# A transformer layer with a routed feed-forward, on one core: the five hand-written orders are laid anew among neighbours

## The chip, the core and the metric

The program runs on one core of a Trainium2 chip. The core has five engines that run their own instruction streams in order: TensorE (PE, matrix products; its weight loads are listed apart as PEld), VectorE (DVE), ScalarE (ACT), GpSimd (POOL) and SyncE (SP), which issues DMAs. They wait for one another through semaphores only. The metric is device time in microseconds. Three runs of the kernel before gave 949.52, 950.03 and 952.06; their median is 950.03 us.

## The reference

Eight images of 1024 tokens with 29 features go through one layer, all in float32:

```python
h = x.reshape(8, 1024, 29) @ W + pe                       # tokens, width 128
z = layernorm(h)
Q, K, V = z @ Wq + bq, z @ Wk + bk, z @ Wv + bv           # 8 heads of 16
attn = softmax((Q @ K.T + causal_mask) / 4)               # causal, 1024 x 1024 per head
h = h + (attn @ V) @ Wo + bo
f = layernorm(layernorm(h)) * ln_scale + ln_bias
shared = swiglu(f @ shared_in.T) @ shared_out.T + b       # hidden width 256
g = argmax(f @ group_gate.T + ...)                        # 2 groups of 4 experts
top-2 of softmax(expert logits of group g), renormalised
he = swiglu(f @ expert_in.T)                              # one hidden layer for all experts
h = h + shared + sum_e weight_e * (he @ expert_out[e].T) + expert biases
```

## The kernel before

**Tiling.** Images are numbered i = 0 to 7. An image has two halves of 512 tokens, and a half has four tiles of 128. Attention of an image is cut into four units (UNITS, four heads times one half of the queries each).

**Steps.** All work is a list of small steps. Each has a letter, which names its stream:

- s, `score` (L546): one 128-query tile of one head against up to 512 keys, 96 steps an image. DVE takes the row maximum from the bank: with the causal mask on the diagonal (L784), without it elsewhere (L780). Two banks, so PE may be two scores ahead of DVE.
- t, `turn` (L559): the maxima of a unit are transposed, split on DVE (L798 to L804) and put into q_stack by SP (L449).
- p, `prob` (L576): keys against queries again, now transposed and with the maximum subtracted, 96 steps an image. ACT takes the exponential into one of four slots `pt` (L1051). Two banks again. On the diagonal POOL zeroes the masked part (`prob` on POOL, L1213), once for each group of four.
- w, `weigh` (L594): four heads' probabilities times values; `take` on ACT (L1042) empties the bank after a unit.
- e, `emb` and a, `stat1`, `turn1`, `ztl`, `q`, `k`, `rest_of`, `v`: embedding and what comes ahead of attention (L508, L516, L480 to L482, L529 on PE; L720 to L770 on DVE; L1023 to L1032 on ACT; L1186 to L1207 on POOL). POOL's `v` (L1194) adds the output bias to h.
- b: behind attention: `to` (L612; L816 and L818 on DVE), `ant` (L616; L1061 on ACT), `oproj` (L622; L825 on DVE), `stat2`, `z2t` (L628; L843, L1067, L1069, L1229), `gates` (L632), `route` parts 0 to 4 on DVE (L872 to L923), `counts` (L638).
- f: `in` (L480 to L482 into bank_f; tanh on ACT L1089, then L936 or L945 on DVE), `hid` (L1097 and L1234), `expert` (L682 to L684; ACT L1107, DVE L955). h: `shared` (L645, L648; DVE L961). c: `combine` (four L1113 on ACT, then L1243, L1247, L1249 on POOL). d, i: transfers of queries and keys, first loads and weights.

**The order.** `streams(i)` gives for every letter the steps of image i in a fixed order, `works` says which engine has a part in a step, and the table `ORDER` holds one string of letters per engine. `woven` takes, letter by letter, the next step of that stream. So a step never passes another of its own letter, but it may stand anywhere among the others, and on each engine at a place of its own. Attention of image i+1 is interleaved with the feed-forward of image i.

**Waits.** Each step waits for the semaphores that it needs. Steps of many kinds on PE write the one bank bank_m; whichever is next waits until the one ahead was taken (`m_free`, counters `m_ready` and `m_taken`). `fill` puts products into the PE stream that nothing reads: ahead of the first steps, one ahead of each of the first scores, and ahead of the last half's `oproj` (5), `z2t` (14) and `gates` (6). A fp32 product is two rows of the trace.

Of the kernel before, what the change touches and what calls it, by code (L numbers as in the profile page):

```python
# [118 lines left out]
def works(engine, i, st):  # L119
# [15 lines left out]
    if engine == "pool":  # L135
# [8 lines left out]
        "eeaaaaessessssassssassssssesssstssasssasssssssssspsspptpssspspppswspasppsspwspsasssppwppssaspspwsspappss"  # L144
        "spspspwppspspspspwptswwassssssspspbpssppbwpspsbsppsapspswssppsspssppswsppsbppspssppappspwwpsstspspwsspas"
        "psbpsswpspspsppspfpswpspfspsafpspfsptspwwwpspsfssppfspspwpspsbppsfspfsppwwpspsfppsbfpspsfspfspsfssppfsps"
        "hssppwwsppsapspsssfssfspswstpswspsasspsswsppsesppspstspsspwpsbpssspsppsspsppspbspspswwwssbwspsbppsspapps"
        "wwpsbsspspbspfpfptsspfpwpwppssfsasfspfpsfspfspsfssfssbwsbspfbssppfsspbspfssbsppsfpspptwwsphpwspbspwpsbpp"
        "sappfppfppfbwwpefpspfsppfssppwppwppsfpspspfpsappsfppsfspafspshsspfspptfswwwpsspfbpsspfbsfbsppsfssbppsfsp"
        "spawsppwspwwpspasppswpsptpssppeppswwppsbspswspsaspsffspbpfsappffpsswspfspfpfbwssppfpspbfbpsspfbfsspbpspf"  # L150
        "sshppssfppbswwswsspptfsppsffppssbspspfsppsfspfsappswwspwspfspspftwspswppsffpsspapspsfpspsasfpssapsfpssbf"
        "spshsftspspfssfpssesfspwwwwsppapspspwspsppassppsswsppsspspswpspwsppsbsppspwpspspbpwpspsptspwpspbpspswsbp"
        "pspspeppspwpspasppwpsspwbspwsspbpspfspfpspffapswwsbfpbfpspbsfpsfbppsfbspspfpsphssppfbfssftspsfssbsppsfsa"
        "sfsppfspasswwwwsppfsppfsstppfpsapsspfsfppssasppsfpssfpspswwwwssppfspspbfpspsfspshpsspwpssfsppsfpspstffsp"
        "sfsspesswwwppssbsppspspbpsspwsppwpspbpsspbpwspwpeppssppaspwpsppspwspptwsppsbswssassfspfafsspfppsbpfspafs"
# [1197 lines left out]
```

## Time and profile before

| | before |
|---|---|
| median of 3 runs | 950.03 us |
| profiled execution | 951.46 us |
| its span | 949.7 us |
| mean granted TensorE clock | 0.984 |
| PE, DVE, ACT, POOL busy | 96%, 83%, 63%, 39% |

The profiled execution took 951.46 us, of which its span (first to last instruction) is 949.7 us and 1.8 us lie around it. PE is busy nearly throughout, so the windows by stage and the waits say more than the shares; they stand in the section of rows.

### The profile page before, as it was taken

Reading aid. Unit: us, or ns where it says so; the run is one execution under the profiler, and the core shown is the slowest. Engines: PE = TensorE matmul, PEld = TensorE weight load, DVE = VectorE, ACT = ScalarE, POOL = GpSimd, SP = SyncE. Lnnn points to the kernel's source line nnn. Section 1 sums busy time; section 2 is a strip of 40 time slices with the busy share of each in tenths; the row PEclk is TensorE's granted clock in tenths of the full one; section 3 lists DMA queues with packets and bytes.
Section 4 is the critical chain, followed back from the end, with each engine's and each line's share of the span. In section 5 each row is a group of like instructions: output and inputs, shape, how many; then the busy total and the mean of one; then the engine's idle time right before and its main releaser. Section 6 shows DMA issues by size and latency. Waiting matters only on the chain. (4 is left out here: it accounts for less than half of the span.)

```text
span 949.7 us, 17664 instructions
## 1 busy us (share of the span) xinstructions
PE 907.3 (96%) x5646; PEld 540.7 (57%) x5646; DVE 786.0 (83%) x2529; ACT 596.3 (63%) x1365; POOL 374.8 (39%) x526
## 2 busy tenths in 40 slices
PE   7788999899999999999999999999999999999996
PEld 7633356356575656457555756466564765555575
DVE  5799988798789888889889889898889998894543
ACT  1335675475857675775766675675767576776644
POOL 3713323323445335343354325344444234332424
PEclk9799999899999999999999999999999999999999
DMA  5231011200111001110102001110110101000000
GB/s 178 59 54 50 20 35 34 65 16 4 34 46 57 10 18 49 38 65 18 35 15 72 26 24 40 45 47 30 38 46 17 47 26 46 26 13 2 12 1 23
DMA packets 45980, 35.19 MB, mean 37 GB/s; under 512 B 10816, under 2 KB 44608, under 8 KB 45760
## 3 DMA queue, kind: packets, MB, share of 16 engines
q1 hardware_dynamic: 43680, 31.97, 10.5%
q10 hardware_dynamic: 2208, 2.10, 1.0%
q8 instruction: 45, 0.74, 0.4%
q14 instruction: 47, 0.39, 0.1%
HBM read 4.28 MB, written 4.19 MB: 9 GB/s over the span
## 5 line engine op out<-in xcount | busy, mean ns | idle before, releaser
L1051 ACT ACTIVATE pt<-bank_p 128x512 f32<-128x512 f32 (+3 forms) x768 | 349.9, 492 | 200.6 <-PE bank_p L576 178.5
L784 DVE CUSTOM_DVE_ANT_0 bank_s<-bank_s,causal 128x384 f32<-128x384 f32 (+3 forms) x512 | 244.3, 505 | 40.0 <-PE bank_s L546 37.2
L546 PE MATMUL bank_s<-k_stack,q_stack 96*128 96x512 bf16 (+3 forms) x768 | 236.0, 333 | 17.4 <-DVE mx L784 8.9
L576 PE MATMUL bank_p<-q_stack,k_stack 99*128 99x512 bf16 (+3 forms) x768 | 229.0, 332 | 6.9 <-ACT pt L1051 5.1
L780 DVE TENSOR_REDUCE mx_far<-bank_s 128x1 f32<-128x512 f32 x256 | 166.0, 682 | 20.6 <-PE bank_s L546 19.2
L1213 POOL TENSOR_SCALAR_AFFINE_SELECT pt<-pt 128x512 f32<-128x512 f32 x128 | 81.1, 636 | 206.7 <-ACT pt L1051 206.5
L594 PE MATMUL bank_w<-pt,v 128*32 128x512 f32 (+3 forms) x1536 | 155.2, 502 | 0.2 <-POOL pt L1213 0.2
L546 PEld LDWEIGHTS bank_s<-k_stack,q_stack 96*128 96x128 bf16 x768 | 72.1, 99 | 131.9 <-DVE mx L784 55.6
L576 PEld LDWEIGHTS bank_p<-q_stack,k_stack 99*128 99x128 bf16 x768 | 72.7, 99 | 117.6 <-ACT pt L1051 69.8
L682 PE MATMUL bank_f<-wex_h,hid_h 128*128 128x512 f32 x256 | 116.4, 455 | 0.8 <-DVE gate L936 0.7
L684 PE MATMUL bank_f<-wex_h,hid_l 128*128 128x512 f32 x256 | 101.4, 396 | 0.0
L683 PE MATMUL bank_f<-wex_l,hid_h 128*128 128x512 f32 x256 | 101.2, 395 | 0.0
L1113 ACT ACTIVATE sel<-sel,wsel 128x128 f32<-128x128 f32 x256 | 81.5, 399 | 15.5 <-DVE sel L955 15.5
L784 DVE DVE_READ_ACCUMULATOR2_ANT mx<- 128x1 f32 x512 | 72.0, 141 | 0.0
L594 PEld LDWEIGHTS bank_w<-pt,v 128*32 128x32 f32 x1536 | 36.4, 109 | 62.5 <-issue 47.4
L1243 POOL TENSOR_TENSOR sel<-sel 128x256 f32<-128x256 f32 x64 | 46.8, 731 | 59.4 <-ACT sel L1113 59.4
L1107 ACT ACTIVATE sel<-bank_f,gm 128x512 f32<-128x512 f32 x64 | 44.0, 687 | 41.5 <-PE bank_f L684 21.8
L480 PE MATMUL bank_f<-z2t_h,win_h 128*128 128x512 f32 x128 | 66.6, 520 | 3.3 <-DVE gate L936 2.0
L1234 POOL TENSOR_TENSOR hid_l<-hid,hid_h 128x512 fp32r<-128x512 f32 x32 | 41.0, 1284 | 71.9 <-ACT hid_h L1097 71.9
L955 DVE SCALAR_TENSOR_TENSOR sel<-bank_f,gm,sel 128x512 f32<-128x512 f32 x64 | 47.7, 746 | 26.1 <-PE bank_f L684 16.5
L682 PEld LDWEIGHTS bank_f<-wex_h,hid_h 128*128 128x128 f32 x256 | 48.4, 189 | 13.2 <-issue 1.4
L684 PEld LDWEIGHTS bank_f<-wex_h,hid_l 128*128 128x128 f32 x256 | 48.1, 188 | 11.2
(139 smaller groups left out, 1428.9 us busy)
## 6 DMA issues: line engine op xcount, KB each, us to landing
q_stack<-qk_h SPq DMA_DIRECT2D x96, 64.0 KB, 2.6
k_stack<-qk_h SPq DMA_DIRECT2D x84, 64.0 KB, 2.6
q_stack<-qk_m SPq DMA_DIRECT2D x64, 64.0 KB, 2.6
out<-h SPq DMA_DIRECT2D x16, 256.0 KB, 2.4
k_stack<-qk_m SPq DMA_DIRECT2D x56, 64.0 KB, 2.6
q_stack<-qk_l SPq DMA_DIRECT2D x32, 64.0 KB, 2.6
k_stack<-qk_l SPq DMA_DIRECT2D x28, 64.0 KB, 2.4
x_sb<-x_t SPq DMA_DIRECT2D x16, 64.0 KB, 2.4
```

The source lines that it names most:

```text
L480: nc.tensor.matmul(dst, wh, xh, start=True, stop=False)
L546: nc.tensor.matmul(s_bank[s % 2][:, 0:cols], q_stack[0:STACK, half, hd, t % HT * P:(t % HT + 1) * P], k_stack[0:STACK, hd, key_place(i, ha ...
L576: nc.tensor.matmul(p_bank[p % 2][:, q0:HALF], k_stack[:, hd, key_place(i, kt // HT), kt % HT * P:(kt % HT + 1) * P], q_stack[:, half, hd, ...
L594: mm = nc.tensor.matmul(w_bank[VW * j:VW * (j + 1), q0:HALF], v[:, i % 2, kt, first:first + VW], pt[:, k % PT_SLOTS, j, q0:HALF], start=(k ...
L682: nc.tensor.matmul(f_bank[g][:], hid_h[:, c, tok], wex_h[:, c, w], start=(c == 0), stop=False)
L683: nc.tensor.matmul(f_bank[g][:], hid_h[:, c, tok], wex_l[:, c, w], start=False, stop=False)
L684: mm = nc.tensor.matmul(f_bank[g][:], hid_l[:, c, tok], wex_h[:, c, w], start=False, stop=(c == HID // P - 1))
L780: nc.vector.tensor_reduce(mx_far[:, u, col:col + 1], s_bank[s % 2][:], AX.X, ALU.max).then_inc(s_taken, 1)
L784: nc.vector.tensor_tensor_reduce(src, src, causal[:, HALF - cols:HALF], 1.0, -3.0e38, ALU.add, ALU.max, mx[:, u, col:col + 1]).then_inc(s_ ...
L1051: nc.scalar.activation(pt[:, k % PT_SLOTS, j, q0:HALF], p_bank[p % 2][:, q0:HALF], ACT.Exp, scale=0.25).then_inc(exp_done, 1)
L1113: nc.scalar.mul(sel[:, t % 2, part], sel[:, t % 2, part], wsel[:, t, e:e + 1]).then_inc(weighted, 1)
L1213: nc.gpsimd.affine_select(out=d, in_=d, compare_op=ALU.is_ge, fill=0.0, base=0, pattern=[[0, G4], [1, P]], channel_multiplier=-1).then_inc ...
```

## The change

Only the table `ORDER` differs. Each of its strings holds the same letters as before, so every product, wait, buffer and transfer is there as before. Counting the steps whose place in their engine's list differs, and the mean distance over all steps of the engine: PE 1123 of 2224 (0.82 places), DVE 426 of 1301 (0.47), ACT 429 of 1142 (0.56), POOL 158 of 318 (0.87), SP 80 of 123 (1.4). Runs of one letter change little: on PE a run of two p's stands 160 times before and 176 times now.

```diff
     "pe": (
-        "eeaaaaessessssassssassssssesssstssasssasssssssssspsspptpssspspppswspasppsspwspsasssppwppssaspspwsspappss"
...
+        "eeaaaaesesssssassssasssssssessstssssassssssssssptspppsspspsspsssppwpppasswpspsaspssppsspasswpsspaspsps"
...
     "sp": (
-        "ieedededtdetdtdddttddddtcddtdetddctddtdctdddetddtcdtedctdddeedtddtdctecddtdddtdtddctdddtedcddteteddcddtt"
...
+        "eiededdtdtddtddtddtddetcteddeddtdctddtdctdddtedddtectdedcdtdeddtddcdttddecteddddtdcdttdddtdcddttddectddet"
...
```

At the start of DVE's stream, the split of the query and key weights (L967, L970) and the first steps of image 0; z is the normalised half. Before:

```order
L967 CAST wqk_h<-z 128x128 x2
L970 TENSOR_TENSOR wqk_l<-z,wqk_h 128x128 x2
L720 TENSOR_TENSOR h<-bank_m,pos_sb 128x512
L726 BN_STATS stats<-h 128x6 x4
L732 BN_AGGR mv<-stats 128x2 x4
L738 TENSOR_SCALAR z<-h,mv,rs 128x128 x4
L720 TENSOR_TENSOR h<-bank_m,pos_sb 128x512
```

Now:

```order
L720 TENSOR_TENSOR h<-bank_m,pos_sb 128x512
L726 BN_STATS stats<-h 128x6 x4
L732 BN_AGGR mv<-stats 128x2 x4
L720 TENSOR_TENSOR h<-bank_m,pos_sb 128x512
L967 CAST wqk_h<-z 128x128 x2
L970 TENSOR_TENSOR wqk_l<-z,wqk_h 128x128 x2
L738 TENSOR_SCALAR z<-h,mv,rs 128x128 x4
```

The weight split moved from ahead of the first embedding to behind the second, and the second embedding moved ahead of the normalisation L738, which it followed. On SP the load of image 1's first half now stands ahead of the ten loads of the remaining weights, and on ACT the fill of three key rows (L1138) stands first instead of between `q` and `k` of the second half.

Near the end of PE's stream, in image 7: two `in` steps, the last two `weigh` steps (L594) and the first `expert` step. Before:

```order
L480 MATMUL bank_f<-z2t_h,win_h 128x512
L481 MATMUL bank_f<-z2t_h,win_l 128x512
L482 MATMUL bank_f<-z2t_l,win_h 128x512
L594 MATMUL bank_w<-pt,v 32x256 x4
L594 MATMUL bank_w<-pt,v 32x128 x4
L480 MATMUL bank_f<-z2t_h,win_h 128x512
L481 MATMUL bank_f<-z2t_h,win_l 128x512
L482 MATMUL bank_f<-z2t_l,win_h 128x512
L682 MATMUL bank_f<-wex_h,hid_h 128x512
```

Now:

```order
L480 MATMUL bank_f<-z2t_h,win_h 128x512
L481 MATMUL bank_f<-z2t_h,win_l 128x512
L482 MATMUL bank_f<-z2t_l,win_h 128x512
L480 MATMUL bank_f<-z2t_h,win_h 128x512
L481 MATMUL bank_f<-z2t_h,win_l 128x512
L482 MATMUL bank_f<-z2t_l,win_h 128x512
L594 MATMUL bank_w<-pt,v 32x256 x4
L594 MATMUL bank_w<-pt,v 32x128 x4
L682 MATMUL bank_f<-wex_h,hid_h 128x512
```

`in` step (3,1) moved ahead of the two `weigh` steps. At the same place of DVE's stream, the gate products L936 and L945 of the `in` steps, `route` part 4 (L914 to L923) and the first `to` (L816, L818). Before:

```order
L936 SCALAR_TENSOR_TENSOR gate<-gate,bank_f 128x512
L914 TENSOR_TENSOR topp<-eprob,top 128x16
L915 TENSOR_REDUCE esum<-eprob 128x4
L917 TENSOR_REDUCE tsum<-topp 128x4
L919 SCALAR_TENSOR_TENSOR tden<-esum,tsum 128x4
L921 RECIPROCAL trec<-tden 128x4
L923 TENSOR_TENSOR wsel<-topp,trec 128x16
L945 SCALAR_TENSOR_TENSOR hid<-gate,bank_f 128x512
L936 SCALAR_TENSOR_TENSOR gate<-gate,bank_f 128x512
L945 SCALAR_TENSOR_TENSOR hid<-gate,bank_f 128x512
L816 RECIPROCAL rec<-bank_m 128x16
```

Now:

```order
L945 SCALAR_TENSOR_TENSOR hid<-gate,bank_f 128x512
L936 SCALAR_TENSOR_TENSOR gate<-gate,bank_f 128x512
L945 SCALAR_TENSOR_TENSOR hid<-gate,bank_f 128x512
L914 TENSOR_TENSOR topp<-eprob,top 128x16
L915 TENSOR_REDUCE esum<-eprob 128x4
L917 TENSOR_REDUCE tsum<-topp 128x4
L919 SCALAR_TENSOR_TENSOR tden<-esum,tsum 128x4
L921 RECIPROCAL trec<-tden 128x4
L923 TENSOR_TENSOR wsel<-topp,trec 128x16
L816 RECIPROCAL rec<-bank_m 128x16
```

The six routing instructions moved behind both L945. POOL's `v` of the last half (L1194) moved 35 places back, behind the last `combine` of image 6.

In the middle of POOL's stream, where image 5's first masks (L1213) begin: a `combine` (L1243 to L1249) and a `rest_of` (L1205, L1207). Before:

```order
L1213 AFFINE_SELECT pt<-pt 128x4x128 x2
L1243 TENSOR_TENSOR sel<-sel 128x256
L1247 TENSOR_TENSOR h<-h,sel 128x128
L1249 TENSOR_TENSOR h<-h,sel 128x128
L1213 AFFINE_SELECT pt<-pt 128x4x128 x4
L1205 CAST qk_m<-qk_r 128x512
L1207 TENSOR_TENSOR qk_l<-qk_r,qk_m 128x512
```

Now:

```order
L1243 TENSOR_TENSOR sel<-sel 128x256
L1247 TENSOR_TENSOR h<-h,sel 128x128
L1249 TENSOR_TENSOR h<-h,sel 128x128
L1213 AFFINE_SELECT pt<-pt 128x4x128 x2
L1205 CAST qk_m<-qk_r 128x512
L1207 TENSOR_TENSOR qk_l<-qk_r,qk_m 128x512
L1213 AFFINE_SELECT pt<-pt 128x4x128 x3
```

The combine stands ahead of image 5's first mask, and the rest_of ahead of its third mask instead of behind the fifth.

## Rows read from the trace of the kernel before

**Rows 1.** Windows: stretch, length, then busy us (instructions) of PE, PEld, DVE, ACT, POOL; clock, DMA share, GB/s.

```profile
0.00:200.00 200.00, 177.26 (x1028) 97.96 (x1028) 165.41 (x527) 98.51 (x204) 73.04 (x94) 0.93 0.21 59
200.00:880.00 680.00, 671.00 (x4289) 399.58 (x4289) 588.93 (x1916) 462.75 (x1074) 273.58 (x389) 1.00 0.10 33
...
897.00:919.00 22.00, 22.00 (x146) 19.64 (x144) 9.03 (x23) 7.14 (x16) 7.44 (x12) 1.00 0.04 14
```

**Rows 2.** Groups by form: busy us, mean ns of one, idle before.

```profile
L1051 ACT ACTIVATE pt<-bank_p 128x512 f32<-128x512 f32 x384 | 216.7, 601 | 91.6 <-PE bank_p L576 84.8 <-PE bank_w L594 5.5
L780 DVE TENSOR_REDUCE mx_far<-bank_s 128x1 f32<-128x512 f32 x256 | 166.0, 682 | 20.6 <-PE bank_s L546 19.2
```

**Rows 3.** Timeline of the start: start us, length, engine, instruction, idle before.

```profile
5.67 0.36 DVE L967 CAST wqk_h<-z 128x128 fp32r<-128x128 f32 x2 [1.64 <-DMA bk_sb<-bk]
...
6.07 0.49 DVE L970 TENSOR_TENSOR wqk_l<-z,wqk_h 128x128 fp32r<-128x128 f32 x2
...
7.65 2.05 PE L508 MATMUL bank_m<-tokw_sb,x_sb 128*128 128x128 f32 x8 [0.95 <-DVE h L720]
...
10.40 1.12 DVE L738 TENSOR_SCALAR z<-h,mv,rs 128x128 f32<-128x128 f32 x4 [1.58 <-POOL rs L1190]
...
12.27 0.63 PE L516 MATMUL bank_m<-ident,z 128*128 128x128 f32 x4
```

**Rows 4.** Timeline, the first two scores and the embedding behind them.

```profile
25.46 0.27 PE L546 MATMUL bank_s<-k_stack,q_stack 96*128 96x128 bf16 x1 [0.83 <-DMA k_stack<-qk_l]
...
26.06 0.31 PE L546 MATMUL bank_s<-k_stack,q_stack 96*128 96x128 bf16 x1
...
28.22 0.69 DVE L720 TENSOR_TENSOR h<-bank_m,pos_sb 128x512 f32<-128x512 f32 x1 [1.99 <-PE bank_m L508]
```

**Rows 5.** Windows of two stretches in image 1's scores.

```profile
181.70:188.50 6.80, 6.60 (x36) 2.56 (x36) 2.59 (x12) 1.55 (x4) 0.63 (x1) 0.50 0.22 70
165.00:180.00 15.00, 12.63 (x70) 4.85 (x66) 14.71 (x38) 7.60 (x19) 8.38 (x12) 1.00 0.22 73
```

**Rows 6.** Timeline of image 5's second and third mask, the third's use, a rest_of.

```profile
607.97 0.64 POOL L1213 TENSOR_SCALAR_AFFINE_SELECT pt<-pt 128x512 f32<-128x512 f32 x1 [1.26 <-ACT pt L1051]
...
610.84 0.64 POOL L1213 TENSOR_SCALAR_AFFINE_SELECT pt<-pt 128x512 f32<-128x512 f32 x1 [2.24 <-ACT pt L1051]
...
612.35 0.64 PE L594 MATMUL bank_w<-pt,v 128*32 128x256 f32 x8
...
615.25 0.61 POOL L1205 CAST qk_m<-qk_r 128x512 bf16<-128x512 f32 x1
615.95 1.16 POOL L1207 TENSOR_TENSOR qk_l<-qk_r,qk_m 128x512 bf16<-128x512 f32 x1
```

**Rows 7.** Timeline around the last two weigh steps.

```profile
894.41 1.27 POOL L1234 TENSOR_TENSOR hid_l<-hid,hid_h 128x512 fp32r<-128x512 f32 x1
894.45 0.86 PE L594 MATMUL bank_w<-pt,v 128*32 128x256 f32 x16
894.62 0.60 ACT L1089 ACTIVATE gate<-bank_f 128x512 f32<-128x512 f32 x1 [0.38 <-PE bank_f L482]
894.70 1.01 DVE L923 TENSOR_TENSOR wsel<-topp,trec 128x16 f32<-128x16 f32 x1
...
895.63 0.68 DVE L945 SCALAR_TENSOR_TENSOR hid<-gate,bank_f 128x512 f32<-128x512 f32 x1
...
896.36 0.50 PE L480 MATMUL bank_f<-z2t_h,win_h 128*128 128x512 f32 x1 [1.05 <-DVE hid L945]
...
897.16 0.39 PE L682 MATMUL bank_f<-wex_h,hid_h 128*128 128x512 f32 x1
```

**Rows 8.** L923 in all: ns min, median, max; first and last start.

```profile
L923 DVE TENSOR_TENSOR wsel<-topp,trec x16: 174/175/1019, 143.6 to 930.8; 128x16 f32<-128x16 f32 x16
```

**Rows 9.** POOL's `v` in all, and DVE's use of the last product of attention.

```profile
L1194 POOL TENSOR_TENSOR h<-h,bo_sb x16: 1263/1288/1327, 15.5 to 796.7; 128x512 f32<-128x512 f32 x16
...
904.94 0.69 DVE L825 TENSOR_TENSOR h<-bank_m,h 128x512 f32<-128x512 f32 x1 [2.54 <-PE bank_m L622]
```

More of the change, by code:

```diff
@@ new lines @@
+        "hspspwwsppsaspsspsfssfsswstswppspsapsssswspspesswppspstsspspppsppssbsppssppppspsbssswwssbwssbspwpspappsp"
+        "wsppbswssbpsfpsspfpftpwpfpspswpsfssapsfpfspsfpsfssfssbwsbspfbpsspfspspbsfpssbspfppsstwpspwphpwpsbswpsbpp"
+        "sappfppfppfbwwpsfpepfpspsfpspwppwppsfpspsfpspasppfppfspsapsfphssfpspstfswwwspspfbsspfpsbfpspsbfspsbsppsf"
+        "psawpwssppwwppsaspspwpspstpsppeppswwppsbspswspsaspsffbspfpsafspfsppwpfsspfpfwspspbfsbpspfbssppfbfpssbspf"
+        "psphwsspfbpsspwwsppstfspsfpfppssbppssfpsspfpsfspapswwspspfswsppftspwpspwpsfasspfpspsfpsapssfspsapssfbpsp"
@@ new lines @@
+        "fsshspsfstfssfppsespfswwwwsppsapssppwpspspassppsswspspssppswssppwpspbspsppwppsspbpwpspstppswpspbsppswsbp"
+        "pspspepspspwppaspspwsppwbpswsspbppfspsfssppfapwwpbfsfbpfssbpfppsfbspfbpspfsppshspfpsbfssftssfpssbsppsfsp"
+        "sapsffpssaswwwwspspfppfssptpfsspasppfsfpspsaspsfpspsfspspwwwwsppsfsbppsfpsspfspsphpsspwssfsppstfpssffpss"
+        "fssppesswwwpspsbspspsppbspspwppbpspwspsbpspspwwpeppssppasppwspsppwsptspwpspbswssassffspapfpsfsbpspffassp"
+        "pfspswpspfwpssbfsbfbspspfbspfbpspsfpphspspfbpswwpssptwspsfspbspspfppsapspfpspswpspswwsppfpfssppftssppfsp"
@@ new lines @@
+        "sappsswwwsppsfsppsfspspfpspaspsfsspfsppsassppfbfsshsspfstfspsfssefspswwppswwspsaspsspswspspasppswpspbpps"
+        "swsppbppspsptpwspspbwpspsbpssppasppwsppwppsasppwpbsppswssbspsfppswpfbspfbspfppbfppsfbsfpsfpsbfppsshpspfb"
+        "ssfssbfpsptfesswwppsswwspsfbppssfppsfasppsffpssppapspsfspwwwssptfsppawspspfspsfpsspapspsfppswwspsfwspspf"
+        "tppsfspsfpspshppssfsppsfppssfssfpspsfspesswwwwssppspssppsbppwpspbpwsppsapswspsppbswsbppssppstppwppsapwpp"
+        "spsppwpspbspswpssaspsfsfppsbspffsspefspspfassppfwwwssppbffspsbfbpspsfbpssfsspphspfsspptfpssbpsspffsapsww"
@@ new lines @@
+        "fssssbsbsstbshsssbbfabsbfffsbssfsfessfssfsafssfasashsssfstssafbsssbssfssbsbfssabssssssastssesssssssasffb"
+        "sbfssffbsfsabfsfbssabssfsbssbsbssfbhsssfsssstassfssfssfssbssfsfssbassbstfsfbsbfssasfssssassasfssssfshsst"
+        "ssfseafssassssassssssssssssassssbsssbsstsssssbssbesssbasssssbbssfsbfbsbafafsbfsfbsfssafbsbfssbhssssfssst"
+        "ssfssbsbsbsabsbfssasfsfsstsfsfsasfssfsssssasfssfsssssfssshssssftssfssssfessasssbssbssasssbbssesssbsassst"
+        "ssssssasfsfasffssbfssasfbsbbsffsbsbsfbsassfbbssbhssasssstfsssssbbssbssfssfasfssfsstssfsfbsabssssfssfsssf"
@@ new lines @@
+        "sasssfasssfshssstssfsseafssasssssssasssassbsssbssstssssbsbsassbassssssbsbbsbfsfbbffsbsfsfssffsbbssbhsfss"
+        "sssbstfbssebabssssbfssasfssassfsfsasfstssfssassfsfssssssafsfstssfssshssfssssfsssssfesassssssabssbsssasss"
+        "ssbssbtssbsasssssssasfsfssbfssfebssfbsfsbfabsfsssbabfssssafssshssstssbfsbssfbasssssssassftfssbssbssbbsba"
+        "ssfsfsfssfssssssfsassfsfsssssfstsshsssssfssssfssbssbsssssbbstsssssbssssssbssbfsbfbfbfssfssfssfssfsssfsss"
+        "fsstbbbbbhfbfbbbffffffffbbfbbbhbfffbfbfbffffbffbffhff"
@@ L199 @@
+        "cfapacccpaacppcpppppppapbabfafappbcbpcpfafpcacpccppcaapppcpbppppbaaffabapcbpcppfcafcpapacpcapcppapppcpbp"
+        "pbffabpabcapcppfafcpcpaccpcapappppppbppcbaaffaaccppbpbpfapcfpapcppccppppcpbppcbffppppbcbcpppfpfccabccbff"
         "cccccc"
```

73 lines of the change are left out of this document (24 added, 49 removed).

## Prediction

> **What bounds the kernel now.** I read three views in this order: the windows by stage, the timelines of the places whose order changes, and the groups by form. The windows show that from 200 to 880 us PE is busy 671.0 of 680 us, so 9.0 us are idle there, and that it is busy all of 897 to 919 [rows 1]. In the first 200 us it is busy 177.26, so 22.7 us are idle, with DVE busy 165.41. So three quarters of the program is bound by PE's own work, which the change leaves as it is (the same products, in another order). What an order can win lies in the idle 22.7 us of the first 200, the 9.0 us of the middle, and a few us at the end. One more loss is no idle time: from 181.7 to 188.5 us the granted clock is 0.50, PE's lower level of 1.2 GHz, and PE is busy 6.60 us with what 3.3 us would do at the full 2.4 GHz [rows 5]. Ahead of it, from 165 to 180, PE was busy only 12.63 of 15 us while DVE was busy 14.71: a stretch in which DVE is the bound.
>
> **Scale.** The profiled execution took 951.46 us (span 949.7 and 1.8 around it), 1.43 above the median 950.03 of the runs. The sum is made on 951.46, and 1.43 is taken off at the end. What the measurement of this kernel can tell from no change is about 0.3%, 2.85 us.
>
> **The change, part by part.**
>
> *Start.* (a) The split of the weights, L967 and L970, runs from 5.67 to 6.56, 0.89 us, ahead of everything else on DVE [rows 3]. It now stands between the second L720 and L738. The first L720 gains nothing by this, since it waits for PE's first product; so the split loses a place where it stood beside that product. PE's second product ends at 9.70 (7.65 + 2.05), and DVE can take its L720 (0.69 us, as at 28.22, [rows 4]) from about 9.8, ending near 10.45, when the factors that L738 waited for until 10.40 are there too. The split then ends at 11.35, and L738 (1.12) at 12.5, against 11.52 before (10.40 + 1.12). PE's L516 stood at 12.27 behind fill products, so it moves to about 12.65: +0.37 us. (b) Before, the second embedding of image 1 began on PE 0.10 us behind the second score of 26.06. Now it stands behind the first, of 25.46: 0.60 us sooner, and DVE had been idle 1.99 us for it until 28.22 [rows 4]. The score moved back costs PE the same where it now stands, so this gains 0.60 only while DVE is what is late, which it is there: -0.6. (c) On SP, the load of image 1 goes ahead of ten loads of weights, which are used twenty us later; on ACT, the fill L1138 goes to an idle start. I count both as 0. Together the start gives -0.2 us; the bounds are +0.4 (only a) and -0.6 (only b).
>
> *The first 200 us otherwise.* Steps there move by about one place on all engines. The far row maximum L780 takes DVE 682 ns and a score needs less on PE; the exponential L1051 takes ACT 601 ns [rows 2]. Where more than two scores stand together on PE, each further one costs up to 0.68 us of waiting for DVE, and each further p up to 0.60 for ACT. I counted runs in both tables: scores beyond the second in a run fall from 29 to 26 in the whole program, -2.0 us at most; p's beyond the second rise from 4 to 7, +1.8 us at most. The two bounds nearly cancel, and other steps stand beside each of these runs in either order: I take 0. DVE's own order is the same in the stretch from 165 to 180, apart from PE's, so I expect its 2.37 us of idle PE (15 - 12.63), and the half clock behind it, to come again [rows 5]. Term 0. The ends: if both go, -2.37 - 3.3 = -5.7 us; if a second such stretch comes, +3.3 with about 2 us of idle time ahead, +5.3.
>
> *The middle.* 9.0 us idle in 680 leave little to win; half of it would be -4.5, and I see no part of the change that collects it. Of what could be lost, the nearest is on POOL, which now has `combine` and `rest_of` ahead of masks that they followed. In image 5, `rest_of` (0.61 + 1.16, from 615.25 to 617.11, 1.86 us) stands ahead of the third mask. That mask began at 610.84 and the one before ended at 608.61 (607.97 + 0.64), so 2.23 us lie open, the 1.86 fit with 0.37 to spare, and the products that use the mask began at 612.35, 0.87 us after it ended at 611.48 [rows 6]. By DVE's order its input is made ahead of the second mask, so it can start at once. So it costs 0; the other end is its whole 1.86. I read the similar places (`combine` ahead of the first mask of image 5, and in image 6) the same way. SP's transfers move by 1.4 places on average; PE's idle 9.0 us leave little room for any wait on them now, and I take 0, with the 1.86 as the nearest size of a loss.
>
> *The end.* Before, DVE did the six instructions of `route` part 4 between L936 and L945 of one `in` step. The last of them, L923, took 1.01 us beside POOL's L1234 (894.41 to 895.68), while its median is 0.175 us [rows 7, 8]. L945 so came at 895.63, and PE's next `in` product, which writes the bank that L945 empties, waited 1.05 us, until 896.36; the last `weigh` had ended at 895.31 (894.45 + 0.86), and the first `expert` product came at 897.16. Now six routing instructions stand behind both L945, and `in` (3,1) ahead of the two `weigh` steps. L945 of (2,1) can come right behind its L936, near 893.5, its L945 be done by 894.2, and the product of (3,1) follow (3,0) without a gap, near 894.5 to 895.3. The `weigh` products (0.86 for the last of them) then end near 896.1. The bank that `expert` writes is emptied behind the gate of (3,0): L1089 until 895.22 (894.62 + 0.60), then L936, as long as L945's 0.68, near 896.0. So `expert` can start at 896.1 instead of 897.16: -1.06 us. From 897 to 919 PE has no idle time [rows 1], so the gain is carried on.
>
> What was moved back has a price too. `route` part 4 is done near 897.8 instead of 895.71 (894.70 + 1.01), and `combine` on ACT and POOL waits for its weights. POOL's `v` of the last half, 1.29 us, stands behind the last `combine` of image 6 now, and is needed by DVE's last L825, at 904.94 [rows 9]. ACT is busy 7.14 and POOL 7.44 of the 22 us from 897 on [rows 1], so both have room: by my count `v` is done near 903, a good 0.8 us before L825 now wants it (904.94 - 1.06 = 903.9), and I take 0. If it is late, it costs up to its own 1.29, which would turn the end into +0.2. So the end lies between -1.06 and +0.2; I take -1.06, as each time of it stands in a row.
>
> A rule of the Trainium skill bears on L923. The row: 1.01 us beside a POOL operation that reads two tiles, 0.175 us at the median of 16 [rows 7, 8]. By "SBUF — State Buffer" (Who interferes with whom) a DVE instruction with two inputs in SBUF and a GpSimd instruction that reads SBUF exclude each other for the whole instruction, and issue order decides who waits. The trace agrees with that here. By the rule, routing moved behind both L945 may meet the next POOL operation in turn, and lose the same 0.84 again; that would be -0.9 for the end instead of -1.1, since only 0.2 of it is on PE's path. The sum below doesn't use it.
>
> **The sum.** Start -0.2, first 200 us otherwise 0, middle 0, end -1.1: -1.3. On the profiled execution 951.46 - 1.3 = 950.2; on the median's scale 950.03 - 1.3 = 948.7 us.
>
> **The rivals.**
>
> *A, the forecast: 948.7, its own range 946.5 to 951.0.* The two placed terms come as worked out and the rest nets out to within 2 us.
>
> *B, faster: the DVE-bound stretch dissolves.* Where PE's order around 165 us puts other work between scores, PE gets back the idle 2.37 and the half clock, 3.3 us, doesn't recur: 948.7 - 5.7 = 943.0. For it: PE's order changes in half of its steps, and 22.7 us of idle time in the first 200 are a large store. Against it: DVE is busy 14.71 of 15 us there and its order is the same, so PE can't get its scores taken sooner. A part of it (the half clock alone) gives 945.4.
>
> *C, slower: a mask comes late.* The place is image 5's third mask behind `rest_of`. If that pair starts later than 609.85 (the mask must start by 612.35 - 0.64 = 611.71, less 1.86), the `weigh` products wait. At worst 1.86 us, and if a half-clock stretch like that of 181.7 follows the gap, 3.3 more: 948.7 + 1.86 + 3.3 = 953.9. For it: 0.37 us to spare is less than what steps move. Against it: the products have 0.87 us more, and a short gap in the middle left the clock at 1.00 before.
>
> *D, the gain isn't there: 950.0.* The 1.06 us at the end is taken back by `v` or `combine` behind it, and the start nets to 0. Then the change does nothing that can be measured.
>
> **Chances.** A 0.42, B 0.25, C 0.22, D 0.11. The bounds of 0.3% lie at 947.2 and 952.9. A falls below 947.2 with 0.11 and is the same with 0.31; B is faster with 0.25; C is slower with 0.20 and the same with 0.02; D is the same with 0.08, slower with 0.03. So faster 0.36, same 0.41, slower 0.23. The range reaches from B's full size to C's: 943.0 to 954.5, with about 0.1 left out at either side.
>
> **What would show it.** Start: L516 of the first half near 12.65, and DVE's wait for the second embedding of image 1 down from 1.99 by 0.6. First 200 us: granted clock 0.50 again for some 6 us behind a stretch from 165 on with DVE at 14.7 of 15. Middle: PE busy near 671 of 680 and no new wait of L594 for POOL's L1213 beyond 0.2 us. End: no idle time of PE between `in` (2,1) and `expert`, which start about 1.1 us sooner relative to 880. The forecast is wrong if the idle time of PE in the first 200 us moves by over 2 us from 22.7, or if a half-clock stretch comes or goes.

## The result and the profile after

Over 20 runs of each, the changed kernel takes 944.43 us in the median (941.3 to 950.8) and the kernel before 950.75 (948.5 to 953.0). The ratio is 0.9944, with a 95% interval of 0.9932 to 0.9956: 5.3 us less (4.2 to 6.5). The forecast was 948.7, within its range of 943.0 to 954.5. The sign and the range held, and the size did not: I had -1.3 us.

The profiled execution took 945.19 us, its span 943.4 us, at a mean granted clock of 0.983 (before 0.984). In the mean of the 20 runs it is 0.983 too, and 0.983 in 86 runs of the kernel before, so the clock isn't what made it faster. Windows of the changed kernel, columns as in [rows 1]; 200 to 880 answers to the row of before there, and 891 to 913 to that of 897 to 919:

```profile
0.00:200.00 200.00, 177.99 (x1034) 97.63 (x1035) 166.79 (x534) 99.04 (x206) 74.53 (x95) 0.93 0.23 61
200.00:880.00 680.00, 673.89 (x4307) 400.71 (x4305) 589.98 (x1919) 467.84 (x1084) 273.89 (x389) 1.00 0.10 33
...
891.00:913.00 22.00, 22.00 (x146) 19.58 (x145) 9.89 (x29) 8.78 (x20) 9.76 (x16) 1.00 0.04 14
```

PE's idle time from 200 to 880 us fell from 9.0 to 6.1 us, in a stretch where I had written 0. To see where time went I set each PE step of one trace against the same step of the other, and took the median difference of the steps in each stretch. A positive number means later than in before:

| steps near (us of before) | changed kernel |
|---|---|
| 25 to 50 | 0.0 (from -0.3 to +0.8) |
| 65 to 77 | +2.5 |
| 100 to 180 | +1.0 to +0.6 |
| 200 | -1.5 |
| 255 | -1.9 |
| 260 | -2.7 |
| 565 | -3.7 |
| 570 | -4.9 |
| 605 | -5.5 |
| 640 to 890 | -5.7 to -5.3 |
| 895 to the end | -6.3 |

The curve falls in steps, with long flat parts between them. The steps at 260, 570, 605 and 895 each stand at one gap of PE in the trace of before. Between 260 and 565 it falls by another 1.0 us, in small pieces at no large gap. The first three of these gaps, with the ACT instruction ahead of two of them (timeline of before, columns as in [rows 3]):

```profile
258.00 0.69 ACT L1032 ACTIVATE qk_h<-bank_m,bk_sb 128x512 bf16<-128x512 f32 x1
...
258.58 0.44 ACT L1051 ACTIVATE pt<-bank_p 128x128 f32<-128x128 f32 x2
...
259.00 0.38 PE L576 MATMUL bank_p<-q_stack,k_stack 99*128 99x512 bf16 x1 [0.68 <-ACT pt L1051]
...
569.57 1.17 POOL L1207 TENSOR_TENSOR qk_l<-qk_r,qk_m 128x512 bf16<-128x512 f32 x1
569.75 1.02 DVE L923 TENSOR_TENSOR wsel<-topp,trec 128x16 f32<-128x16 f32 x1
...
571.82 0.34 PE L546 MATMUL bank_s<-k_stack,q_stack 96*128 96x384 bf16 x1 [0.99 <-DVE mx L784]
...
605.91 0.69 ACT L1032 ACTIVATE qk_h<-bank_m,bq_sb 128x512 bf16<-128x512 f32 x1 [1.30 <-DMA q_stack<-qk_l]
...
607.03 0.34 PE L576 MATMUL bank_p<-q_stack,k_stack 99*128 99x384 bf16 x1 [0.92 <-ACT pt L1051]
```

At 258 us ACT evacuates k, 0.69 us, ahead of an exponential that PE waits for, and PE stands 0.68 us. At 570 the last instruction of `route` part 4 takes 1.02 us beside POOL's L1207, as it did near 895 beside L1234 [rows 7, 8]. At 606 ACT waits 1.30 us for a transfer with exponentials queued behind it. A fourth gap of the same size stands at 297, where PE waits 0.74 us for the transfer `q_stack<-mrow_l`. The changed kernel has it too (0.70), so it is in neither's favour. The same places in the changed kernel:

```profile
566.08 0.17 DVE L923 TENSOR_TENSOR wsel<-topp,trec 128x16 f32<-128x16 f32 x1
566.17 0.42 DVE L784 CUSTOM_DVE_ANT_0 bank_s<-bank_s,causal 128x256 f32<-128x256 f32 x1
566.33 0.74 POOL L1243 TENSOR_TENSOR sel<-sel 128x256 f32<-128x256 f32 x1 [2.44 <-ACT sel L1113]
...
566.93 0.34 PE L546 MATMUL bank_s<-k_stack,q_stack 96*128 96x384 bf16 x1
...
600.37 0.69 ACT L1032 ACTIVATE qk_h<-bank_m,bq_sb 128x512 bf16<-128x512 f32 x1 [0.67 <-DMA q_stack<-qk_l]
...
601.49 0.34 PE L576 MATMUL bank_p<-q_stack,k_stack 99*128 99x384 bf16 x1 [0.36 <-ACT pt L1051]
```

L923 is back at 0.17, with no POOL instruction beside it, and the score behind it has no idle time. The gap at 606 is down to 0.36. The end of attention, which answers to [rows 7]:

```profile
889.33 0.60 ACT L1089 ACTIVATE gate<-bank_f 128x512 f32<-128x512 f32 x1 [0.23 <-PE bank_f L482]
889.56 0.40 PE L482 MATMUL bank_f<-z2t_l,win_h 128*128 128x512 f32 x1
889.88 0.86 PE L594 MATMUL bank_w<-pt,v 128*32 128x256 f32 x16
889.96 0.69 DVE L936 SCALAR_TENSOR_TENSOR gate<-gate,bank_f 128x512 f32<-128x512 f32 x1 [1.03 <-ACT gate L1089]
...
890.79 0.47 PE L682 MATMUL bank_f<-wex_h,hid_h 128*128 128x512 f32 x1
```

`in` (3,1), the weigh products and `expert` follow without idle time. `expert` starts at 890.79, against 897.16 before. All of 6.37 us less the 5.3 that steps at 880 had is 1.07: the term of the end as forecast, 1.06.

### The profile page after: what moved, and what is told of

Its sections match the earlier page's. It is cut to its first block, busy times and chain, and to the rows that moved or that the text cites. A ratio compares the mean times of both kernels' runs of the same rounds, so it can differ in the third digit from the quotient of the medians.

```text
span 943.4 us, 17664 instructions
## 1 busy us (share of the span) xinstructions
PE 905.6 (96%) x5646; PEld 539.0 (57%) x5646; DVE 785.6 (83%) x2529; ACT 597.1 (63%) x1365; POOL 376.1 (40%) x526
## 4 chain that ended last, share of the span: by engine, by line
PE 85%; DVE 9%; ACT 2%; issue 1%; DMA 1%; SPq 0%; ACTq 0%; POOL 0%; POOLq 0%; DVEq 0%
PE bank_w L594 13%; PE bank_p L576 13%; PE bank_s L546 13%; PE bank_f L682 6%; PE bank_f L683 6%; PE bank_f L684 6%; PE bank_f L480 3%; PE bank_f L482 3%; PE bank_f L481 3%; PE bank_m L648 3%; DVE bank_s L784 3%; DVE mx_far L780 3%; PE bank_m L508 2%; PE bank_m L622 2%; PE bank_m L612 1%; PE bank_m L632 1%
## 5 line engine op out<-in xcount | busy, mean ns | idle before, releaser
L546 PE MATMUL bank_s<-k_stack,q_stack 96*128 96x512 bf16 (+3 forms) x768 | 238.8, 336 | 15.6 <-DVE mx L784 7.5
L1213 POOL TENSOR_SCALAR_AFFINE_SELECT pt<-pt 128x512 f32<-128x512 f32 x128 | 82.1, 642 | 217.5 <-ACT pt L1051 217.4
L594 PE MATMUL bank_w<-pt,v 128*32 128x512 f32 (+3 forms) x1536 | 154.7, 497 | 0.3 <-ACT ot L1042 0.2
L684 PE MATMUL bank_f<-wex_h,hid_l 128*128 128x512 f32 x256 | 101.3, 396 | 0.0
L1234 POOL TENSOR_TENSOR hid_l<-hid,hid_h 128x512 fp32r<-128x512 f32 x32 | 41.1, 1285 | 108.4 <-ACT hid_h L1097 108.4
L1243 POOL TENSOR_TENSOR sel<-sel 128x256 f32<-128x256 f32 x64 | 46.9, 733 | 59.4 <-ACT sel L1113 59.4
L594 PEld LDWEIGHTS bank_w<-pt,v 128*32 128x32 f32 x1536 | 35.4, 108 | 59.2 <-issue 45.7
L684 PEld LDWEIGHTS bank_f<-wex_h,hid_l 128*128 128x128 f32 x256 | 48.1, 188 | 11.2
```

The lines of the kernel that those rows point to most:

```text
L546: nc.tensor.matmul(s_bank[s % 2][:, 0:cols], q_stack[0:STACK, half, hd, t % HT * P:(t % HT + 1) * P], k_stack[0:STACK, hd, key_place(i, ha ...
L594: mm = nc.tensor.matmul(w_bank[VW * j:VW * (j + 1), q0:HALF], v[:, i % 2, kt, first:first + VW], pt[:, k % PT_SLOTS, j, q0:HALF], start=(k ...
L684: mm = nc.tensor.matmul(f_bank[g][:], hid_l[:, c, tok], wex_h[:, c, w], start=False, stop=(c == HID // P - 1))
L1213: nc.gpsimd.affine_select(out=d, in_=d, compare_op=ALU.is_ge, fill=0.0, base=0, pattern=[[0, G4], [1, P]], channel_multiplier=-1).then_inc ...
```

## The experiments

The difference that moves the time is small, so two measures stand side by side: the ratio of many runs, and the curve of steps of one trace. Where two programs have the same order the curve mostly stays level within 0.1 us over hundreds of us. It isn't always so: waits for a transfer come and go between traces of the same order. The one at 297 stands in the trace of before and not in e3's. One of 0.97 us at 506 stands in e1's trace and one of 0.79 in e7's, and in neither before nor e3. A step of one trace at such a place is not an effect of the order.

The ratio is an estimate of its own over the runs, and not the quotient of the two means (for e1 that quotient is 0.9985, for e9 0.9983). e3, e5 and e6 ran once each, for the trace, so of them only steps are read. The others (mean and standard deviation of the times, ratio to before with its interval, number of runs):

| kernel | mean us | sd | ratio | runs |
|---|---|---|---|---|
| before | 950.7 | 1.1 | | over 80 |
| changed | 945.3 | 2.6 | 0.9944 (0.9932 to 0.9956) | 20 |
| e1, new up to 200 us | 949.3 | 2.3 | 0.9979 (0.9964 to 0.9994) | 12 |
| e7, new up to 57 us | 949.7 | 1.7 | 0.9992 (0.9979 to 1.0005) | 12 |
| e8, new from 57 to 200 | 950.7 | 2.9 | 0.9999 (0.9979 to 1.0019) | 12 |
| e2, new from 200 to 880 | 948.5 | 1.3 | 0.9979 (0.9968 to 0.9990) | 12 |
| e12, four single moves | 947.7 | 0.8 | 0.9967 (0.9956 to 0.9978) | 12 |
| e9, changed without these | 948.9 | 2.8 | 0.9976 (0.9962 to 0.9990) | 12 |
| e10, changed, 57 to 200 old | 947.0 | 0.9 | 0.9962 (0.9950 to 0.9974) | 5 |
| e4, changed with fills | 945.5 | 1.7 | 0.9944 (0.9927 to 0.9960) | 6 |
| e11, changed with 4 swaps | 946.5 | 3.0 | 0.9958 (0.9939 to 0.9977) | 12 |

Within a kernel the time follows the clock of the run: over the 20 runs of the changed kernel the fastest took 941.3 us at a clock of 0.989 and the slowest 950.8 at 0.973. One line through all runs, with a level for each kernel, gives 0.47 us for each 0.001 of clock (0.3 to 0.7 in one kernel alone, and no slope in e12's runs). Where "at equal clock" stands below, the level of this line at 0.984 is meant, with two standard errors.

**By stretches.** e1, e2 and e3 take the new orders in one stretch each. In each string of `ORDER` a piece is taken from the new table only where it holds the same letters as the old one, so all else stays. e1:

```diff
     "pe": (   # all pieces up to 200 us, on all five engines
-        "eeaaaaessessssassssass...
+        "eeaaaaesesssssassssass...
```

> The kernel before with the new orders of all engines only up to 200 us (the places are taken by the times of its trace), the old ones behind. Theory G (gaps: the change wins by gaps of PE that vanish at single places, most of them behind 200 us): this kernel stands within 2 us of before, with steps at 200 us from 0 to 1.6 us earlier and no difference that grows behind. Rival C (clock: the change wins by half-clock stretches of the first 200 us that shrink): the whole gain is here, 4 to 6 us.

Measured 0.9979, -2.0 us (-3.4 to -0.6), and -1.3 +- 0.6 at equal clock. That is within the 2 us of theory G and far from C's 4 to 6. C falls: the gain is not all in the first 200 us. G's second sign is not borne out: in e1's trace, which is of its slowest run, the steps at 200 us come 0.6 later than in before, and not 0 to 1.6 sooner.

e2 has the pieces from 200 to 880 us:

```diff
-  pieces of before, 200 to 880 us
+  pieces of the changed kernel, 200 to 880 us
   (but POOL: ..."apcpp", the piece that moves v(7,1), as before)
```

> The kernel before with the new orders only from 200 to 880 us, without the one long piece of POOL's order that moves the last v. Theory G: the PE gaps at 258.3 (0.68), 570.8 (0.99) and part of that at 606.1 (0.92 to 0.36) vanish, steps at 880 us come 3.0 to 3.8 us earlier than in before when the first 200 us are set equal; the time falls by about 3.5 us, 0.37%. Rival C: 0 to 1 us. My prediction on record had 0 for this stretch.

The steps at 880 us come 3.2 us sooner than in e3, whose orders there are the old ones, when both are set equal at 200 us. The gaps at 258 and 571 are gone, and that at 606 is 0.69. The time fell by 2.0 us (3.0 to 1.0), at equal clock 2.3 +- 0.6. So G holds in kind, with a size from 2.0 (times; 2.3 at equal clock) to 3.2 us (steps of one trace), at the lower end of its 3.0 to 3.8 or below it. My 0 for the middle is wrong by either.

e3 has the new orders from 880 us on (42 letters), without the move of v. The part at 895:

```diff
-  PE  ... w w in(3,1) expert        DVE ... route4 in(2,1) in(3,0) in(3,1)
+  PE  ... in(3,1) w w expert        DVE ... in(2,1) in(3,0) in(3,1) route4
```

> The kernel before with the new orders only from 880 us on. By the forecast's term of the end the first expert product behind the last weigh comes 1.06 us sooner relative to steps at 875 us, and stays so to the end; route part 4's L923 takes 0.175 us. If the place of POOL's v mattered (it is not moved here), the end would differ from the changed kernel's by more than 0.2.

The steps behind 895 us come 0.98 us sooner relative to those at 880. The end of the changed kernel has 1.0 too, so the place of v gives and costs nothing.

**Single moves.** e5 puts four single moves, each of one engine alone, into the kernel before; 12 letters differ:

```diff
 ACT, 258 us:   - k(2,1)  prob(23,2)
                + prob(23,2)  k(2,1)
 POOL, 569 us:  - rest_of(0,1) hid(0) hid(1) prob combine(6) rest_of(1,1) combine(7)
                + hid(0) combine(6) rest_of(0,1) hid(1) combine(7) prob rest_of(1,1)
 ACT, 603 us:   - take(3) prob(0,3) prob(1,0)
                + prob(0,3) prob(1,0) take(3)
 DVE, 894 us:   - route(0,4) in(2,1) in(3,0) in(3,1)
                + in(2,1) in(3,0) in(3,1) route(0,4)
```

> The kernel before with four single moves of the change, each on one engine alone, so that each place speaks for itself. (1) ACT near 258 us: the evacuation of k (L1032, 0.69) behind one exponential instead of ahead of it; theory: PE's gap of 0.68 is just this length and goes; rival: it needs the moves of PE too and stays. (2) POOL near 569 us: hid and combine ahead of rest_of; theory: L923 was slow (1.02) only because rest_of's L1207 ran beside it, so it takes 0.175 now and PE's gap of 0.99 shrinks by 0.85; rival: the gap is of DVE's order (route ahead of the gate product), and stays over 0.8. (3) ACT near 603 us: two exponentials ahead of take; theory: PE's gap of 0.92 at 606 falls by up to 0.56; rival: it hangs on the transfer of queries that L1032 waits for (1.30), and stays. (4) DVE near 895 us: route part 4 behind the gate products of in; theory: PE's gap of 1.05 goes with this alone, and expert comes 1.06 sooner.

Against e3 the curve falls by 0.62 at 258, 0.97 at 571 and 0.41 at 606, and against before by 1.00 at 895. Between these places it is level within 0.1 us (for instance -3.10 at 260 and -3.19 at 560). Timeline of e5 at 567 us and at 891 us:

```profile
566.60 0.18 DVE L921 RECIPROCAL trec<-tden 128x4 f32<-128x4 f32 x1
566.67 0.28 PE L546 MATMUL bank_s<-k_stack,q_stack 96*128 96x256 bf16 x1
566.81 0.17 DVE L923 TENSOR_TENSOR wsel<-topp,trec 128x16 f32<-128x16 f32 x1
566.90 0.68 DVE L936 SCALAR_TENSOR_TENSOR gate<-gate,bank_f 128x512 f32<-128x512 f32 x1
...
890.05 0.86 PE L594 MATMUL bank_w<-pt,v 128*32 128x256 f32 x16
890.84 0.50 PE L480 MATMUL bank_f<-z2t_h,win_h 128*128 128x512 f32 x1
...
891.68 0.47 PE L682 MATMUL bank_f<-wex_h,hid_h 128*128 128x512 f32 x1
```

DVE's order at 567 is that of before, only POOL's differs, and L923 takes 0.17 us instead of 1.02: the slow instruction was a matter of what POOL did beside it. The other traces say the same: with POOL's old order there it took 1.02 us in all seven, and with the new one under 0.19 in all seven. Near 891 PE's order is that of before (`weigh` ahead of `in`), only DVE's differs, and the gap of 1.05 us is gone all the same. The page "SBUF — State Buffer" of the Trainium skill (Who interferes with whom) has a DVE instruction with two SBUF inputs and a GpSimd instruction that reads SBUF shut each other out. The trace agrees: 1.02 and 1.01 us beside L1207 and L1234, 0.174 to 0.177 in all 16 executions of the changed kernel. The size of the step at 606 is less sure than the other three. The gap there is 0.55 to 0.97 us in the seven traces with ACT's old order, and 0.35 to 0.69 in six with the new one. The same kernel traced again (e12) has it at 0.60 and a step of 0.15, where e5 has 0.35 and 0.41.

e6 gives the other engines' parts of the same places to the kernel before:

```diff
 PE, DVE, ACT, 566 to 571 us: as changed; POOL as before
 SP: the piece of 15 transfers of images 5 and 6 as changed
 PE, 895 us:    - weigh(22) weigh(23) in(3,1)
                + in(3,1) weigh(22) weigh(23)
```

> The kernel before with the other engines' parts of the same places. (1) PE, DVE and ACT near 566 to 571 us as in the change, POOL as before: if the slow L923 beside POOL makes the gap, something of it stays (over 0.4, L923 or another instruction long); if DVE's order does, it goes. (2) SP's piece of 15 transfers of images 5 and 6 as in the change: by the rival of the transfer, ACT's wait of 1.30 for q_stack<-qk_l near 606 falls to 0.7 and PE's gap from 0.92 to near 0.4; by the theory of ACT's order nothing changes. (3) PE alone near 895 us, in (3,1) ahead of the two weigh: L945 still stands behind the slow route part, so PE waits for it ahead of in, and the weigh products come behind: expert 0.8 to 0.9 us later than in before.

(1) The gap at 571 stays, 0.98 us, and L923 takes 1.02: the rival of DVE's order falls. (2) The gap at 606 stays at 0.80 and ACT's wait for the transfer at 1.2, so it isn't SP's order of transfers. (3) The steps behind 895 come 2.5 us later than at 880, three times what I expected. Timeline and windows of e6 there:

```profile
894.78 1.00 DVE L923 TENSOR_TENSOR wsel<-topp,trec 128x16 f32<-128x16 f32 x1
...
896.44 0.50 PE L480 MATMUL bank_f<-z2t_h,win_h 128*128 128x512 f32 x1 [1.83 <-DVE hid L945]
...
897.34 0.95 PE L594 MATMUL bank_w<-pt,v 128*32 128x256 f32 x16
...
898.22 0.79 PE L682 MATMUL bank_f<-wex_h,hid_h 128*128 128x512 f32 x1
898.39 0.59 ACT L1042 COPY ot<-bank_w 128x512 f32<-128x512 f32 x1 [2.93 <-PE bank_w L594]
898.87 1.28 ACT L1113 ACTIVATE sel<-sel,wsel 128x128 f32<-128x128 f32 x4
899.24 0.63 PE L684 MATMUL bank_f<-wex_h,hid_l 128*128 128x512 f32 x1
```

```profile
894.60:897.30 2.70, 0.87 (x4) 0.49 (x3) 2.35 (x4) 0.75 (x2) 1.15 (x1) 1.00 0.00 0
897.30:901.00 3.70, 3.70 (x24) 2.52 (x24) 0.69 (x1) 1.77 (x5) 0.73 (x1) 0.59 0.02 4
```

Behind 1.83 us of idle PE the mean granted clock is 0.59 over 3.7 us. Within it the clock stands at 0.50, its lower level, for 3.41 us from 897.97 on, and L684 takes 0.63 us instead of 0.40. e9's trace has the same (1.88 us idle, then 3.41 us at 0.50). Behind the gap of 1.05 in before, the clock stayed at 1.00 [rows 1]. So of the 2.5 us that PE's move costs without DVE's, 0.8 is the longer gap (1.83 less 1.05), and 1.7 is the work that PE didn't get done at that clock (3.41 x 0.50).

e12 is e5's kernel, timed:

> The kernel of e5_singles once more, now timed: the kernel before with the four single moves (12 letters differ). Its steps came 3.05 us sooner behind 240 us than in a kernel with the same first 200 us. Theory G: the time is 2.5 to 3.5 us less than before, a ratio of 0.9963 to 0.9974, and the spread is that of before (standard deviation near 1.1), as the orders from 57 to 200 us are the old ones. Rival: single profiles overstate it, as in e9_undo4 (5.3 us of steps, 3.6 in the mean of the times), and it is 1.5 to 2.5 us.

0.9967, -3.1 us (-4.2 to -2.1), with a spread of 0.8. At equal clock it is -2.3 +- 0.6. Theory G's 2.5 to 3.5 is met by the ratio and the rival's 1.5 to 2.5 by the other measure, so the runs don't separate the two. Four moves in 12 letters, of 1,864 places that differ in the whole change, give between two and three fifths of its gain.

e9 is the changed kernel with the four moves undone:

```diff
 the four pieces of e5 in the changed kernel: new -> old
```

> The changed kernel with the four moves of e5_singles undone and all else as changed. In e5 they gave 3.05 us of steps (0.62 at 258, 0.98 at 571, 0.41 at 606, 1.00 at 895) against a kernel of the same first 200 us. Theory G: they carry that in the changed kernel too, so this one takes 2.5 to 3.5 us more than the changed kernel, 947.5 to 948.7 at its mean, and the PE gaps stand there again. Rival: the orders round about were made to fit, so that undone moves cost more than they gave (over 4), or the other moves cover them (under 1.5).

The ratio is 0.9976, 3.6 us in the mean over the changed kernel, with an uncertainty of about 2 (3.4 at equal clock). That is at the upper edge of theory G's 2.5 to 3.5, and its uncertainty takes in the rival of over 4. The trace, which is of its slowest run, has the steps 0.5 later at 258, 0.7 at 571, 0.6 at 606 and 3.5 at 895, the last because PE's move at 895 is in and DVE's is not, as in e6. These make 5.3 us, more than the mean shows. The idle time at 895 and the clock behind it stand in both traces with PE's move alone, e6's and e9's. Whether they come in every run, these can't tell.

**The first 200 us.** e7 has the new orders up to 57 us, 26 letters, e8 those from 57 to 200 us, 326 letters.

```diff
 e7: pieces up to 57 us      new
 e8: pieces from 57 to 200   new
```

> The kernel before with the new orders up to 57 us only. The step to L516 was 0.16 us later in the changed kernel, the first score 0.4 later, and steps at 50 us 0.3 sooner: theory A, this part is worth -0.3 to +0.3 us and leaves the spread of the times as in before (standard deviation 1.1 us over its runs). Rival: it is what widens the spread (2.3 us over the runs with the new first 200 us) by setting when the clock falls.

> The kernel before with the new orders from 57 to 200 us only. Theory A: the 1.3 us that the new first 200 us are worth at equal clock are here, as PE's waits for far maxima (L780: 4.5 us in before, 1.2 in the changed kernel) go, and the spread is here too. Rival: it is worth nothing by itself, 950.5 within 1.

e7 is inconclusive by its ratio (-0.8 us, -2.0 to +0.5), and -1.0 +- 0.6 at equal clock. e8 gives nothing in the mean: theory A's "here" is wrong. What e8 does is spread: 945.5 to 954.5 us. e10 tests this in the changed kernel, with the old orders from 57 to 200 us.

```diff
 e10: the changed kernel, pieces from 57 to 200 us   new -> old
```

> The changed kernel with the old orders from 57 to 200 us. By e8_from57 this part gives nothing in the mean at equal clock, and widens the spread (standard deviation 3.0 us over its 12 runs, 1.1 for before). Theory S: mean within 1 us of the changed kernel's 945.3, spread under 2 us. Rival: the spread comes from other parts (the start, or chance), and stays at 2.5 us or more.

The spread fell to 0.9, with only 5 runs, and the mean is 1.7 higher than the changed kernel's, not within 1, with an uncertainty of 1.5. Over all kernels, those with the new orders from 57 to 200 us spread by 2.3 to 3.0 us, and by 1.7 with e4's fills. Those with the old ones there spread by 0.8 to 1.7. So theory S holds for the spread, as far as so few runs tell; its statement on the mean isn't shown. The spread goes with the clock of the run, in e8 as in the changed kernel. Each profile of the study shows 4 to 6 stretches of granted half clock in the first 200 us, from 3.4 to 17 us long. They differ in place and length even between programs whose orders there are the same. In the changed kernel's profile one of them runs from 55 to 69 us, where the steps fell 2 us behind before.

e4 tried to hold the clock there with products that nothing reads:

```diff
-                if i == 0 and s < UNIT_S[1]:
+                if i == 0 and s < UNIT_S[1] + 16:
                     fill(f_bank[0], 1)
```

> The changed kernel with one product more that nothing reads ahead of each of 16 further scores of image 0 (33rd to 48th, about 55 to 75 us). A fill takes PE about 0.21 us at full clock (11.6 us for 55 of them in a stretch of before at partly half clock), so 16 add up to 3.4 us of PE's work, part of it in PE's gaps there. Theory F (fills hold the clock): the stretch at half clock from 55 to 68 us of the changed kernel's profile, which cost some 3 to 4 us, is gone or shorter, and the time is 0 to 3 us lower. Rival: DVE is the bound there, PE only works more, the clock falls elsewhere, and the time is the same or up to 3 us higher.

In e4's profile the stretch at 55 us is gone, but one of 3.4 us stands at 81, and one near 180 is 10.2 us long instead of 3.4. Its ratio is that of the changed kernel, 0.9944, so the rival's "the same" stands: with the fills half-clock stretches stand at other places, and 6 runs show no gain.

**Four more swaps.** e11 applies what e5 showed to gaps that the changed kernel still has:

```diff
 ACT, 601 us:  - q(6,0) prob(1,1)      + prob(1,1) q(6,0)
 ACT, 704 us:  - take(3) prob(0,2)     + prob(0,2) take(3)
 PE, 508 us:   - score(72) weigh(7)    + weigh(7) score(72)
 PE, 826 us:   - score(71) prob(7,1)   + prob(7,1) score(71)
```

> The changed kernel with four more single swaps of the kind that e5 showed, at PE gaps that it still has: ACT, the evacuation of q behind one exponential (gap 0.36 at 601) and take behind one exponential (0.35 at 704); PE, a score that waits for DVE behind the next weigh (0.45 at 508) and behind the next prob (0.41 at 826). Theory: each gap goes, 1.0 to 1.5 us less in all. Rival: the swap only moves the wait by one step, 0 to 0.3 us less, or what is put behind comes late and it is slower.

The rival won. Against the changed kernel's trace the steps lost 0.5 us at 508, 0.2 at 601, 0.3 at 704 and nothing at 826, 1.0 in all, and the mean is 1.2 higher, inside its uncertainty of about 2. At 508 the swap made two gaps (0.67 and 0.57) of one of 0.45: the swapped-in weigh waited too, for POOL's mask L1213. At 704 the gap stayed (0.39), and at 601 and 826 it went and the steps came no sooner for it. A gap is not by itself an invitation to swap its two neighbours: what is moved ahead must be ready, and what stands behind must not wait for the same thing.

## Why the prediction was right or wrong

**The bound, right.** PE's own work bounds three quarters of the kernel, and the change had only gaps and clock to win.

**The end, right in size, half right in cause.** Forecast -1.06, measured -1.07 in the changed kernel, -0.98 in e3 and -1.00 in e5. I had counted `in` ahead of `weigh` on PE as a part of it. e5 shows that DVE's move alone does it, and e6 that PE's move alone costs 2.5 us. By the Trainium skill's rule I had allowed for L923 meeting the next POOL operation in turn; it didn't, since it took 0.174 to 0.177 in all 16 executions.

**The middle, the step that failed.** I wrote: "The middle. 9.0 us idle in 680 leave little to win; half of it would be -4.5, and I see no part of the change that collects it", and took 0. Measured -2.3 +- 0.6 (times at equal clock) to -3.2 us (steps). I had looked at averages (steps move by 0.8 places, runs of one letter change little) and at what might be lost on POOL. I hadn't taken PE's largest gaps one by one. Of the idle 9.0 us, 2.6 stood in three gaps of 0.68, 0.99 and 0.92, and the order at each shows what the change does. The single moves at these three give 2.0 us in e5's steps and 1.7 in e12's. The other 1.2 to 1.5 of the 3.2 were not taken apart, and they are hardly idle time: from 200 to 880 us PE is idle 8.1 us in e3, 6.2 and 6.4 in e5 and e12, and 5.9 in e2. What they are stays open.

At 570 I had the mechanism in hand from the end of the program: L923 beside a POOL instruction with two inputs. The row of all its executions gives only the maximum, 1019 ns [rows 8]; a list of its executions shows two of over 1 us, and the other one is in the middle.

**The first 200 us, wrong in size.** I had -0.2 for the start and 0 for the rest. At equal clock e1 gives -1.3 +- 0.6, e7 -1.0 and e8 +0.3 (both +- 0.6), so what gain there is lies in the start. Term (a) was near: L516 came at 12.43 (forecast 12.65, before 12.27). Of term (b), DVE's wait for the second embedding of image 1 fell from 1.99 to 1.55 us, by 0.44 where I had 0.60. But the embedding itself came at 28.10 instead of 28.22, only 0.12 us sooner, since the first score stood behind a later transfer (25.90 instead of 25.46). So the traces don't show the two placed terms as a gain, and where the gain of the start comes from stays open.

**The stretch from 165 us and its half clock.** I expected it to come again, and it did in every profile of the study. In that of the changed kernel it is shorter (3.4 us from 178 on, against 6.8 from 181.7 on [rows 5]):

```profile
178.00:182.00 4.00, 3.96 (x15) 1.87 (x14) 3.25 (x6) 1.31 (x5) 2.44 (x4) 0.57 0.17 52
```

That is part of the step from +0.6 to -1.5 near 185. Since another stretch was longer in the same profile (55 to 69) and the mean clock is the same, rival B does not explain the gain, though its 943.0 is close to what was measured. In all, PE has 27.3 us at half clock in the first 200 in either profile.

**The two signs of being wrong.** The idle time of PE in the first 200 us went from 22.7 to 22.0, so it didn't move by 2. Half-clock stretches did come and go: that at 89 us is gone, and that of 3.4 us at 62 is one of 13.7 from 55. But neither sign can judge the forecast. e3, whose orders there are those of before, has 25.0 us idle and other stretches again.

**The masks of rival C.** In before PE's L594 waited once for POOL's L1213, 0.2 us. In the changed kernel no such wait stands in the list of waits from 200 to 874 us, which is:

```profile
PE bank_p L576 <- ACT pt L1051: 1.5, 6, 0.4
PE bank_s L546 <- DVE mx_far L780: 1.2, 4, 0.4
PE bank_p L576 <- DMA q_stack<-mrow_l: 0.7, 1, 0.7
PE bank_s L546 <- DVE mx L784: 0.5, 2, 0.3
PE bank_w L594 <- ACT ot L1042: 0.2, 1, 0.2
```

The wait for ACT's exponentials was 3.9 us, 12 times, in the same part of before; it is 1.5, 6 times. So `combine` and `rest_of` ahead of masks cost nothing, as I had it.

**What moving back costs at the end.** v ended at 897.78 (896.50 + 1.28) and L825 came at 898.66: 0.88 us to spare, where I had a good 0.8.

```profile
896.50 1.28 POOL L1194 TENSOR_TENSOR h<-h,bo_sb 128x512 f32<-128x512 f32 x1
898.66 0.69 DVE L825 TENSOR_TENSOR h<-bank_m,h 128x512 f32<-128x512 f32 x1 [2.87 <-PE bank_m L622]
```

**The sum.** At equal clock the three stretches give -1.3, -2.3 and (by steps) -1.0, together -4.6, against -5.3 +- 0.5 for the whole. They add up within their uncertainty. That the total came out within the range owes something to luck: the forecast's -1.3 is its end term and a -0.2 for the start that the traces don't show, and the larger part of the gain lies where it had 0.

## What to carry to other kernels

Where the main engine is 98% busy, list its gaps by size and read for each the order around it, before and after: here three of its four largest made up 2.6 of its 9.0 idle us, and told more than all averages. Much of what a change in order pays or costs stands at a handful of places, so undo or apply it place by place. Several places fit in one kernel, since between them the curve of steps is mostly level. But trace a kernel twice: waits for transfers (0.74 us at 297, 0.97 at 506) come and go without any change. When a short instruction is slow once, look for all its slow executions and for what ran beside them on GpSimd.

## What the runs showed that was not expected

A change of order can leave the mean as it is and more than double the spread: with the new orders from 57 to 200 us (e8) the standard deviation was 2.9 us against 1.1, nearly all of the excess with the clock of the run. A gap of 1.83 us of PE near 895 us was followed by 3.4 us at a granted clock of 0.50 (and one of 1.88 in e9 too), while a gap of 1.05 at the same place left it at 1.00, so that a wait 0.8 us longer cost 2.5 us. And the orders of two engines at one place belong together: PE's move at 895 is worth nothing with DVE's (e3 -0.98, e5 -1.00) and costs 2.5 us without it (e6).
